# Centring moved into the weights, norms by mean square, and 64-row products on both halves of TensorE

## The reference

```
h = x @ Win.T + bin                              # 512 -> 64 channels
for l in range(4):
    y = silu(layernorm(h, ln1_w, ln1_b))
    y = sconv(y, phazor, last_conv)              # a linear recurrence over the 512 tokens
    h = h + y * sc_lin
    y = layernorm(h, ln2_w, ln2_b)
    y = silu(y @ W1.T + b1) @ W2.T + b2          # 64 -> 256 -> 64
    h = h + y
h = layernorm(h, lnl_w, lnl_b)
y = h @ Wout.T + bout                            # 64 -> 512
```

## Time and profile before

| | |
|---|---|
| profiled execution, time | 2330.87 us |
| span in the trace | 2329.2 us |
| median of three runs | 2328.26 us |
| PE busy | 2211.0 us, 95% |
| DVE busy | 1427.9 us, 61% |
| ACT busy | 1236.2 us, 53% |
| POOL busy | 512.7 us, 22% |
| chain that ended last | PE 81%, DVE 7%, ACT 4%, DMA 3% |
| first to last norm on ACT (L1637) | 24.2 to 281.4 us |

### The profile page before, as it was taken

The page is one execution under the profiler, slowest core; times in us unless marked ns, Lnnn a source line. Parts: engine busy times, 40 slices in busy tenths (PEclk is TensorE's granted clock), DMA queues, the critical chain, the costliest instruction groups (busy, mean ns, idle before and its releaser), DMA issues.

```text
span 2329.2 us, 35733 instructions
## 1 busy us (share of the span) xinstructions
PE 2211.0 (95%) x12523; PEld 1174.1 (50%) x12528; DVE 1427.9 (61%) x3153; ACT 1236.2 (53%) x2313; POOL 512.7 (22%) x646
## 2 busy tenths in 40 slices
PE   6788889999999999999999999999999999999998
PEld 5555444555455454555555555554543444444443
DVE  6757779857667586787878787878732221221212
ACT  5566688657557475676767666778751101011010
POOL 3533233223213122232323231223220000000000
PEclk8789899999999999999999999999999999999999
DMA  6001243313213132332423243333231000000000
GB/s 184 1 1 38 83 130 123 122 42 111 80 48 118 34 119 64 105 102 70 134 66 104 68 128 108 121 101 99 71 94 59 5 14 0 18 0 5 14 0 18
DMA packets 135777, 163.24 MB, mean 70 GB/s; under 512 B 42272, under 2 KB 97696, under 8 KB 135328
## 3 DMA queue, kind: packets, MB, share of 16 engines
q1 hardware_dynamic: 135600, 160.97, 22.4%
HBM read 94.19 MB, written 53.35 MB: 63 GB/s over the span
## 4 chain that ended last, share of the span: by engine, by line
PE 81%; DVE 7%; ACT 4%; DMA 3%; issue 3%; SPq 1%; POOL 1%; POOLq 0%; ACTq 0%; DVEq 0%
PE ps L1543 16%; PE ps L1441 8%; PE ps L1471 8%; PE ps L1554 8%; PE ps L1426 7%; PE ps L1450 7%; PE ps L1496 5%; PE ps L1396 3%; PE ps L1401 3%; PE ps L1505 2%; PE ps L1528 2%; PE ps L1315 2%; PE ps L1481 2%; DVE peaks L2151 2%; PE ps L1407 2%
## 5 line engine op out<-in xcount | busy, mean ns | idle before, releaser
L2151 DVE TENSOR_REDUCE peaks<-ps 128x4 f32<-128x512 f32 x960 | 624.6, 681 | 223.3 <-PE ps L1396 119.7
L1738 ACT ACTIVATE big<-ps 128x512 f32<-128x512 f32 x960 | 546.8, 602 | 247.7 <-PE ps L1426 242.1
L1966 POOL TENSOR_SCALAR_AFFINE_SELECT big<-big 128x512 f32<-128x512 f32 x384 | 257.2, 682 | 897.4 <-ACT big L1738 895.9
L1543 PE MATMUL ps<-xt,big 128*128 128x512 f32 x896 | 390.3, 593 | 2.9 <-issue 2.9
L1426 PE MATMUL ps<-big 99*128 99x512 bf16 (+3 forms) x1536 | 339.9, 302 | 11.8 <-DMA big<-scr_shift 5.8
L1543 PEld LDWEIGHTS ps<-xt,big 128*128 128x128 f32 x896 | 168.8, 190 | 208.9 <-issue 207.7
L1847 ACT ACTIVATE t<-ps 128x512 f32<-128x512 f32 x56 | 33.5, 598 | 452.6 <-PE ps L1543 452.6
L1471 PE MATMUL ps<-xt,big 128*128 128x512 f32 x480 | 248.4, 610 | 2.5 <-ACT xt L1753 2.3
L1441 PE MATMUL ps<-big,vs 128*32 128x512 f32 (+3 forms) x3072 | 241.8, 442 | 7.0 <-POOL big L1966 6.4
L1726 ACT ACTIVATE ps<-cbf 128x512 f32<-128x512 bf16 x384 | 232.5, 606 | 24.6 <-DVE peaks L2151 22.6
L2207 DVE SCALAR_TENSOR_TENSOR t<-rest,t 128x512 f32<-128x512 f32 x56 | 38.7, 691 | 283.9 <-PE ps L1543 282.8
(11 more groups left out here) (232 smaller groups left out, 2955.1 us busy)
## 6 DMA issues: line engine op xcount, KB each, us to landing
big<-scr_q SPq DMA_DIRECT2D x96, 384.0 KB, 3.9
scr_q<-big SPq DMA_DIRECT2D x48, 384.0 KB, 2.7
scr_q<-big SPq DMA_DIRECT2D x48, 256.0 KB, 2.9
recb<-scr_sums SPq DMA_DIRECT2D x96, 128.0 KB
big<-scr_k SPq DMA_DIRECT2D x48, 192.0 KB, 3.2
big<-in_ffn_gu SPq DMA_DIRECT2D x14, 512.0 KB, 5.4
scr_q<-big SPq DMA_DIRECT2D x48, 128.0 KB, 2.8
ctxt<-ots SPq DMA_DIRECT2D x192, 32.0 KB, 2.0
```

The lines of the kernel that those rows point to most:

```text
L1543: mm = pe.matmul(bank_of(kind, n, m), wgu[:, m // 2, c, way, m % 2 * P:(m % 2 + 1) * P], xt[:, c, :], start=(c == 0), stop=(c == DC - 1))
L1738: act.activation(probs[:, place(g, i) * S:(place(g, i) + 1) * S], bank_of("exp", g, i), ACT.Exp, scale=1.0 / 16 if attn_of(n) == 1 else 0. ...
L1966: pool.affine_select(block_, block_, [[0, GQ], [1, P]], ALU.is_ge, zero, base=0, channel_multiplier=-1).then_inc(made["cut"], 1)
L2151: dve.tensor_reduce(to, blocks, AX.X, ALU.max, negate=True).then_inc(made["negmax"], 1)
```

## The change

- **Centring.** The mean over the 64 channels is taken out of all that is added to h instead of out of h: `centre_in` (DVE) centres the weights and bias of the way in, `centre_out` (DVE) those of `narrow`, and the selection that adds the recurrence, `sel2`, is made of the unit matrix minus 1/64. So h has mean zero at all times. `centre_in` stands in front of the first `project_in`, `centre_out` in front of the first `narrow`; both need their weights to have landed.
- **Norms.** ACT squares h from PSUM to SBUF in one ACTIVATE of 128 x 256 (`squares_h`, semaphore `hq`). DVE sums the squares in one TENSOR_REDUCE and scales the sum in one small instruction (`h_squares`, `hs`). POOL takes the power (`h_rstd`, one instruction, `hr`). DVE multiplies h by it in one TENSOR_TENSOR of 128 x 512 (`norm_h`, `hx`). ACT's four ACTIVATEs, four BN_STATS and four BN_AGGR, one small instruction on DVE and one on POOL are gone.
- **64-row products.** `widen` for k = 0 takes rows 0 to 63 of weights and u, for k = 1 rows 64 to 127, where the second half of W1 is now loaded. `project_out` takes rows 0 to 63 for even groups of tokens and 64 to 127 for odd ones. The two products of a pair write different banks, as before.
- **DMAs.** The layers' weights come in three DMAs instead of one, `wout` in two.
- **Order.** The durations given to `Flow` follow the new steps, and the orders of all engines are made anew.

The orders differ up to step 490 of PE's list of 3882; the last 3392 steps are the same. In front of the first `exp` product PE's list holds the same steps as before but for three that now come behind it: two maxima of the second pair of heads and one leading-out product of batch 2.

The diff, cut to its core (`...` marks what is left out; the planner's table shows two of its lines):

```diff
@@ -134,11 +134,11 @@ def arrived():
-    items = [("tab", 0), ("sel",)]
+    items = [("centre_in",), ("tab", 0), ("sel",)]
...
-    return items + [("tab", m) for m in range(1, 10)]
+    return items + [("tab", m) for m in range(1, 10)] + [("centre_out",)]
@@ -275,7 +275,7 @@ def pieces(kind, k):
     if kind == "hln":
-        return [("DVE", "hs", k, 1350), ("POOL", "hr", k, 1350), ("ACT", "hx", k, 1640)]
+        return [("ACT", "hq", k, 480), ("DVE", "hs", k, 620), ("POOL", "hr", k, 1150), ("DVE", "hx", k, 750)]
...
-        return [("PE", "f", k, 870), ("ACT", "ft", k, 620)]
+        return [("PE", "f", k, 250 if k[2] else 870), ("ACT", "ft", k, 620)]
...
@@ -1053,12 +1057,12 @@
+        hq = [f[:, 0:256] for f in hf]
...
@@ -1278,7 +1282,9 @@
-            load("layers", (lw, ins["ssm_lw"].rearrange("l p n -> p l n")), (e2[:], ins["ssm_e2"]))
+            slw = ins["ssm_lw"].rearrange("l p n -> p l n")
+            load("layers", (lw[:, :, 0:135], slw[:, :, 0:135]), (lw[64:P, :, 135:263], slw[0:64, :, 135:263]),
+                 (lw[:, :, 263:391], slw[:, :, 263:391]), (e2[:], ins["ssm_e2"]))
@@ -1346,11 +1352,13 @@
             def widen(l, q, k):
                 pe.wait_ge(made["ut"], counted("ut", l, q, 1))
-                pe.matmul(bank_for("f", l, q, k), lw[:, l, 7 + P * k:7 + P * (k + 1)], u[q], start=True, stop=True
+                rows = slice(64 * k, 64 * (k + 1))
+                pe.matmul(bank_for("f", l, q, k), lw[rows, l, 7 + P * k:7 + P * (k + 1)], u[q][rows], start=True, stop=True
                           ).then_inc(made["f_full"], 1)
...
             def project_out(b, j):
...
-                pe.matmul(bank_for("last", b, j), u[b][:, j * P:(j + 1) * P], wout, start=True, stop=True
+                rows = slice(64 * (j % 2), 64 * (j % 2 + 1))
+                pe.matmul(bank_for("last", b, j), u[b][rows, j * P:(j + 1) * P], wout[rows], start=True, stop=True
                           ).then_inc(made["y_full"], 1)
@@ -1630,13 +1639,14 @@
-            def norm_h(l, q, k):
-
-                act.wait_ge(made["hr"], counted("hr", l, q, k))
-                for j in range(TJ):
-                    last = act.activation(hn[q][:, j], h[q][:, j].unsqueeze(1).broadcast_to((P, 2, 64)), ACT.Identity,
-                                          bias=hsm[:, q, 3, j:j + 1], scale=hsm[:, q, 2, j:j + 1])
-                last.then_inc(made["hx"], 1)
+            def squares_h(l, q, k):
...
+                act.activation(hq[q], ps[:, H_BANKS[q], 0:256], ACT.Square).then_inc(made["hq"], 1)
@@ -1927,16 +1937,13 @@
             def h_rstd(l, q, k):
                 pool.wait_ge(made["hs"], counted("hs", l, q, k))
-                pool.tensor_tensor(hsm[:, q, 2], hsm[:, q, 1], half[:], ALU.pow).then_inc(pool_links, 1)
-                pool_linked[0] += 1
-                pool.wait_ge(pool_links, pool_linked[0])
-                pool.tensor_tensor(hsm[:, q, 3], hsm[:, q, 0], hsm[:, q, 2], ALU.mult).then_inc(made["hr"], 1)
+                pool.tensor_tensor(hsm[:, q, 2], hsm[:, q, 1], half[:], ALU.pow).then_inc(made["hr"], 1)
@@ -2110,21 +2117,32 @@
-            def h_stats(l, q, k):
...
+            def h_squares(l, q, k):
+
+                dve.wait_ge(made["hq"], counted("hq", l, q, k))
+                then(dve.tensor_reduce(hsm[:, q, 0], hq[q].rearrange("p (j d) -> p j d", d=64), AX.X, ALU.add))
+                dve.tensor_scalar(hsm[:, q, 1], hsm[:, q, 0], 1.0 / 64, EPS, ALU.mult, ALU.add).then_inc(made["hs"], 1)
+
+            def norm_h(l, q, k):
+                dve.wait_ge(made["hr"], counted("hr", l, q, k))
+                dve.tensor_tensor(hn[q], h[q].unsqueeze(2).broadcast_to((P, TJ, 2, 64)), hsm[:, q, 2].unsqueeze(2).unsqueeze(3).broadcast_to((P, TJ, 2, 64)),
+                                  ALU.mult).then_inc(made["hx"], 1)
+
+            def centre(of, at, n):
+
+                means = centres[:, at:at + n]
+                then(dve.tensor_reduce(means, of, AX.X, ALU.add))
+                return dve.scalar_tensor_tensor(of, means.unsqueeze(2).broadcast_to((P, n, 64)), -1.0 / 64, of, ALU.mult, ALU.add)
+
+            def centre_in():
+                dve.wait_ge(weights["in"], 32)
+                centre(wf[:, 3584:3904].rearrange("p (c n) -> p c n", n=64), 0, DC + 1).then_inc(made["centre_in"], 1)
+
+            def centre_out():
+                dve.wait_ge(weights["layers"], 128)
+                for k in range(2):
+                    centre(lw[:, :, 263 + 64 * k:263 + 64 * (k + 1)], 5 + NL * k, NL)
+                centre(b2, 5 + 2 * NL, NL).then_inc(made["centre_out"], 1)
@@ -2384,9 +2402,10 @@
-                    last = dve.tensor_scalar(sel2[:, l, :], e2[:], lw[:, l, 4:5], None, ALU.mult)
+                    last = dve.tensor_scalar(sel2[:, l, :], e2[:], -1.0 / 64, lw[:, l, 4:5], ALU.add, ALU.mult)
```

More of the change, by code:

```diff
@@ L289, in pieces @@
     if kind == "last":
-        return [("PE", "last", k, 870)]
+        return [("PE", "last", k, 250 if k[1] % 2 else 870)]
     if kind == "qm":
         return [("PE", "qm", k, 880), ("ACT", "y16", k, ROWS_ACT)]
-    if kind in ("sel", "begin", "half_bias"):
-        return [("DVE", kind, (), {"sel": 1000, "begin": 3000, "half_bias": 250}[kind])]
+    if kind in ("sel", "begin", "half_bias", "centre_in", "centre_out"):
+        return [("DVE", kind, (), {"sel": 1000, "begin": 3000, "half_bias": 250, "centre_in": 1100, "centre_out": 2800}[kind])]
     if kind == "decode":
@@ L389, in order_of @@
         return [("mod", k), ("sel", ())]
-    if name == "sel":
-        return [("x_in", (1,))]
+    if name == "centre_in":
+        return [("win_in", ())]
+    if name in ("sel", "centre_out"):
+        return [("x_in", (2,))]
     if name == "begin":
@@ L400, in order_of @@
     if name == "hd":
-        return [("ft", k + (1,))]
+        return [("ft", k + (1,)), ("centre_out", ())]
     if name == "last":
@@ L1289, in _ @@
                              ins["fp4_scales"][8 * c:8 * c + 8, :].unsqueeze(1).broadcast_to((8, 16, D))))
[L1290 removed]
+            load("out", (wout[0:64], ins["ssm_wout"][0:64]), (wout[64:P], ins["ssm_wout"][0:64]), (lnl[:], ins["ssm_lnl"]),
                  (bias_of["last"], ins["ssm_bout"].broadcast_to((P, D))))
@@ L1324, in project_in @@
             def project_in(b):
-                pe.wait_ge(weights["in"], 32)
+                pe.wait_ge(made["centre_in"], counted("centre_in"))
                 pe.wait_ge(made["inx"], counted("inx", b, DC - 1))
@@ L1353, in narrow @@
                 pe.wait_ge(made["ft"], counted("ft", l, q, 1))
+                pe.wait_ge(made["centre_out"], counted("centre_out"))
                 pe.matmul(h[q], ident[:], b2[:, l, :].unsqueeze(1).broadcast_to((P, TJ, 64)), start=False, stop=True,
@@ L1364, in project_out @@
                 pe.wait_ge(made["ut"], counted("ut", NL, b, 0))
-                pe.wait_ge(weights["out"], 48)
-                pe.matmul(bank_for("last", b, j), u[b][:, j * P:(j + 1) * P], wout, start=True, stop=True
+                pe.wait_ge(weights["out"], 64)
+                rows = slice(64 * (j % 2), 64 * (j % 2 + 1))
+                pe.matmul(bank_for("last", b, j), u[b][rows, j * P:(j + 1) * P], wout[rows], start=True, stop=True
                           ).then_inc(made["y_full"], 1)
@@ L1688, in turned_h @@
                 if l == NL:
-                    act.wait_ge(weights["out"], 48)
+                    act.wait_ge(weights["out"], 64)
                     act.activation(u[q], bank, ACT.Identity, bias=lnl[:, 1:2], scale=lnl[:, 0:1]
@@ L1692, in turned_h @@
                     return
-                act.wait_ge(weights["layers"], 96)
+                act.wait_ge(weights["layers"], 128)
                 if k == 0:
@@ L1929, in last_bias @@
             def last_bias(b, j):
-                pool.wait_ge(weights["out"], 48)
+                pool.wait_ge(weights["out"], 64)
                 pool.wait_ge(made["inx_full"], counted("inx_full", b, DC - 1))
@@ L2111, in tables_d @@
                 dve.tensor_scalar(i2, c[0], 2.0, None, ALU.mult).then_inc(made["tab_d"], 1)
-            def h_stats(l, q, k):
-                if k:
-                    dve.wait_ge(made["hm_full"], counted("hm_full", l, q))
-                elif l:
-                    dve.wait_ge(made["hd_full"], counted("hd_full", l - 1, q))
-                else:
-                    dve.wait_ge(made["inh_full"], counted("inh_full", q))
-                for j in range(TJ):
-                    last = dve.bn_stats(hstat[:, q, j, :], h[q][:, j])
-                then(last)
-                for j in range(TJ):
-                    last = dve.bn_aggr(hmv[:, q, j, :], hstat[:, q, j, :])
-                then(last)
-                dve.tensor_scalar(hsm[:, q, 0], hmv[:, q, :, 0], -1.0, None, ALU.mult)
-                dve.tensor_scalar(hsm[:, q, 1], hmv[:, q, :, 1], EPS, None, ALU.add).then_inc(made["hs"], 1)
+            def h_squares(l, q, k):
[18 more added lines that the diff above has]
```

(13 more changed lines are left out.)

26 lines of the change are left out of this document (16 added, 10 removed).

## The result

The changed kernel takes 2314.78 us (median; 2308.61 to 2322.14), the kernel before 2328.41 in the same comparison. The ratio is 0.995, with a 95% interval of 0.9934 to 0.9966: faster by half a per cent. The forecast was 2313.6. The profiled execution has a span of 2318.5 us, against 2329.2.

The account below looks back on a forecast made before the run. It took a chain over all engines, PE the fullest, to bound the stretch to the first exponential. Terms -7.2 + 3 - 2 - 10.5 - 1.5 + 2 + 1.5 = -14.7 us gave 2313.6 us against the median; range 2295 to 2331.

Parts of the forecast that it names:

- Where the gain can come from: Stretch from 80 to 284 us: only an earlier start of the stream behind it can gain; the end moves with it.
- the terms of this part are -4.7 us: Norms and centring: -7.2 for norms, +3 for multiplications queued on DVE, -2 for ACT and POOL, +1.5 for centring.
- The number on the path, six: Batch 0, whose end releases the attention: six norms count from its modulation on, each 1.20 us shorter, 7.2 us less.
- forecast 6 in five: DVE between sum and multiplication: stands 1.2 us for POOL in five places, 6 us in all, taken as hidden.
- the 3 us charged for multiplications behind another batch's modulation: DVE's order: two of six norm multiplications stand behind another batch's whole modulation, 2 x 1.5 = 3 us more.
- the 2 us for ACT and POOL: ACT and POOL: less norm work, so one batch's steps no longer stand behind another's norm; 2 us less.
- the centring's 1.5: Tables' part before DVE's first modulation: 3.5 us of new DVE instructions, partly hidden; 1.5 us more.
- DVE doesn't set the pace: Denies the rival that DVE sets the pace, so PE's and ACT's savings don't arrive: -2.2 us, 2326 us; chance 0.25.
- forecast 1.5: Behind 284 us: two more pairs of leading-out products take about 2.3 us instead of 4.34; 1.5 us less.
- the 2 us of mode changes: PE going between whole and half rows: 22 pairs x 2 x 0.1 us, half on the path; 2 us more.
- I count half: 10.5 us less: 64-row products from 80 to 284 us: 21 us less on PE, half counted because PE has 39 us idle.
- its slower rival: Shorter products leave PE more idle, its mean clock from 80 us falls from 0.88 to 0.70: 2341 us; chance 0.07.

Follow-up runs that it names:

- e6: Changed kernel with 88 further transposes of the identity on TensorE ahead of five of its longest waits for a norm's multiplication; 2325.23 us, ratio 0.9985.
- e2: Changed kernel with whole 128-row products and the planner's costs and loads of before for them, norms and centring as changed; 2308.51 us, ratio 0.9924.
- e12: Kernel with new norms, whole products and old planner costs, with GpSimd's power of each norm done twice; 2321.91 us, ratio 0.9968 against 0.9924 without.
- e8: Kernel before with 73 transposes of the identity on TensorE ahead of eleven waits, no norm changed; 2326.02 us, ratio 0.9979.
- e10: Kernel before with the 64-row products but its own planner costs, so its own order on every engine; 2352.91 us, ratio 1.0097.
- e5: Changed kernel, same order and planner costs, but both products of a pair read all 128 rows, the other half's weights zero; 2319.56 us, ratio 0.9956.
- e3: Changed kernel, same order, but both products of a pair take rows 0 to 63, so they can't run at once; 2346.59 us, ratio 1.0053.
- e9: Changed kernel with 64-row products but the planner's old product costs, giving the order made for whole products with those costs; 2316.04 us, ratio 0.995.
- e4: Changed kernel with GpSimd's bias additions for the last projection planned only after the vector engine's opening of the attention's part; 2337.61 us, ratio 1.0032.

## Why the prediction held in the number and not in its reasons

**Where the gain can come from.** Right in the main: it is an earlier start of the exponentials. Over all fourteen profiled executions the start moves by 44 us (264.0 to 307.6) and the distance from it to the end by 16 (2038 to 2055 us), so single steps of a few us, such as e6's, don't show at the end. In the table the starts follow the clock column far more than PE's busy time, which lies between 148.6 and 159.8 in all of them.

**Norms.** The direction is right, the size too small: the terms of this part are -4.7 us, and e2 gained 17.7. One norm got 1.43 us shorter (4.28 - 2.85), where the forecast had 1.20: Square took 0.38 us, not 0.50. The number on the path, six, may be too small as well: e12 gives 10 us for 1.06 us of power and 0.08 of gap more per norm, which would be nine (4 to 14), what its lower clock cost included. Nine by 1.43 are 13 us of the 17.7; the rest may be ACT's and POOL's relief, the order, or the clock, which no run separates. The clock is not all of it: e8, with the old norms, has e2's clock over all executions (0.982 and 0.981) and gains 4.9 us.

**DVE's order and its waits for POOL.** The wait is 7.8 us in 11 places, forecast 6 in five. No run tests the 3 us charged for multiplications behind another batch's modulation, nor the 2 us for ACT and POOL. The first modulation at 42.24 us (forecast 41 to 43, before 40.53) agrees with the centring's 1.5. DVE doesn't set the pace: in e10 it has the kernel before's instructions in the same order, none slower by design, and the kernel loses 23 us over products on PE.

**64-row products.** This step failed. The durations are nearly right: a pair of widening takes 1.42 us in the mean (forecast 1.31) and 1.20 at full clock where a whole one takes 1.94, so the halves run at once. With leading-out, PE has 18 us less to do at the same order (e5), forecast 21. Behind 284 us nothing is saved (4.43 us, before 4.34), forecast 1.5. For the 2 us of mode changes no run speaks clearly: by the profile's modelled ends the next product comes 0.1 us later behind a pair of halves than behind a whole one. The Trainium skill's rule that tiles on different rows run at once (TensorE: Matmul & The Clock Gate, Part 3: Packing small matmuls — row/col tiling) agrees with the 1.20 us. But "I count half: 10.5 us less" took the clock as given. It is the other way at two of three orders: the 64-row products went with a clock of 0.72 for 0.88 and 0.79 for 0.95, and the kernel lost 23 us and 6, the 6 at the edge of its intervals. The prediction had this as its slower rival and gave it 0.07. Its argument against, "work and time shrink together, so PE's share stays near 80%", is right about the share and wrong about what follows: in e10 PE was busy 151.46 of 184 us, before 148.61, and the clock fell all the same. So "shorter products leave PE more idle" isn't the reason either. In e3 the clock stood at 0.50 for 64 us while PE was busy for 57.43 of them. What makes it fall stays open; the runs show that it goes with the 64-row products. In the changed kernel the clock stayed at 0.88, and there the products gained 0.06%, not 10 us. The rival was right in its direction for this part, if not in its mechanism, and not for the whole kernel.

**What the sum left out.** The new costs of the products gave the planner another order. e2 against e5, both with whole products, puts its price at 0.32% or 7.5 us (uncertain by 5). The forecast read two places of the order on DVE and charged 3 us.

**The 5.8 us given back behind 267 us.** PE's busy time by its clock from 284 to 400 us is 106.45 x 0.94 = 100.1 us of full speed after and 104.80 x 0.99 = 103.8 before, so up to 3.7 of the 5.8 may be the clock there. That is argued from windows of two single executions, not tested.

Together: the norms -17.7 (e2), the new order +7.5 (e5), the products -1.4, which is -11.6 us; forecast -4.7, nothing, -10.5 - 1.5 + 2 = -10. Taken in another order (e9 before the order), it is -17.7 for the norms, +6 for the products and nothing for the order: with 64-row products the two orders are equal at 0.995. Either way the sum came out right by luck: the norms' term was too small, the products' term had the wrong sign or far too large a size, and the two errors cancelled.

## What to carry to other kernels

Measure each part of a change alone at the same order of instructions before its gain is believed: here one part alone beat the whole, and the part with the clearest saving on the fullest engine made the kernel before 1% slower. Where TensorE's granted clock moves between its levels, a saving of its busy time is no saving of time until the clock column of the same windows has been read, and the clock of more than one execution. When a planner decides the order, the costs written into it are a change of their own and want a run of their own.

## What was not expected of the hardware

- With the same order and nearly the same durations, products on 64 of 128 rows went with a granted clock of 0.69 from 80 to 264 us, products on all rows, half of whose weights are zero, with 0.87 (e3, e5; over all executions 0.965 and 0.976). The two levels are 1.2 and 2.4 GHz. In e3 PE was busy 10.00 of 10 us in each window from 120 to 140 us, and the clock was 0.50:

```profile
120.00:130.00 10.00, 10.00 (x28) 6.09 (x28) 2.09 (x5) 3.22 (x5) 1.01 (x1) 0.50 0.00 0
130.00:140.00 10.00, 10.00 (x37) 8.02 (x36) 1.87 (x5) 1.46 (x3) 2.02 (x2) 0.50 0.00 0
```

- Two float32 products of 512 columns on the two halves of the rows take 1.20 us together at full clock and 2.15 at half, whole ones 1.94 and 3.69.
- DVE instructions with two operands in SBUF took 1.64 us beside GpSimd's additions and 0.69 without them (e4). The norm's multiplication, which reads PSUM, took 0.68 to 0.69 in all 36 places, beside them too.
- A Square of 256 columns from PSUM on ACT takes 0.38 us; the ACTIVATE of that width in the earlier trace rows, which reads SBUF, took 0.50.
